# A zero fill in pieces, late expert rows copied by ScalarE, and slots moved by one

## The reference

```
# layer 0: every token against every text token, through a tanh of 256 features
h   = tanh(text @ Ws + ln(x) @ W + b)          # [b, 1024, 77, 256]
rho = h . w ; att = softmax(rho + mask)
x   = x + tanh(g) * (tanh(att.text . Wcw) * ln(x) + tanh(att.text . Wcb))
x   = x + tanh(g) * (ln(x) @ (W + low rank).T + b)
# layer 1: attention of 16 heads over the text, then a mixture of experts
x   = x + tanh(g) * (softmax(q k / 4) v @ Wo)  # q from ln(x), k and v from text
r   = top 4 of 16 experts by sigmoid(ln(x) @ router), in the 2 best of 4 groups
x   = x + tanh(g) * (sum over r of tw * (silu(x Wg) * (x Wu)) Wd  + shared expert)
```

## Time and profile before

| | us |
|---|---|
| median of 3 runs | 1641.26 (1637.31 to 1642.3) |
| profiled execution | 1636.88 |
| its span | 1635.1 |
| TensorE busy | 1297.0 (79%) |
| ScalarE busy | 1061.4 (65%) |
| VectorE busy | 979.4 (60%) |
| GpSimd busy | 593.8 (36%) |
| the chain that ended last: TensorE, VectorE, ScalarE, issue, GpSimd, DMA | 36%, 24%, 16%, 8%, 7%, 6% |

### The profile page before, as it was taken

One profiled execution on the slowest core, in us unless ns is written; L12 is line 12 of the kernel. 1 busy time (PEld: TensorE's weight loads), 2 busy tenths in 40 slices (PEclk: granted clock), 3 DMA queues, 4 the chain that ended last, 5 costly groups with the idle time before them and its releaser, 6 DMA issues.

```text
span 1635.1 us, 34527 instructions
## 1 busy us (share of the span) xinstructions
PE 1297.0 (79%) x11876; PEld 763.6 (47%) x11876; DVE 979.4 (60%) x2357; ACT 1061.4 (65%) x1739; POOL 593.8 (36%) x557
## 2 busy tenths in 40 slices
PE   4776377787579989997899889968998787688860
PEld 2211033133134745564556455646476576467750
DVE  7896137644864476458744785598438858223433
ACT  3999376997569979887699788966984241122110
POOL 2100021022273221233732435328335562735536
PEclk9877688899689999999999999999999999899995
DMA  6757700000123353244443544534437655559974
GB/s 180 226 193 183 171 1 26 14 13 27 33 91 78 104 131 98 71 117 123 149 92 107 141 148 127 135 104 141 110 92 184 170 123 137 167 138 229 253 207 119
DMA packets 227796, 202.55 MB, mean 124 GB/s; under 512 B 116747, under 2 KB 185523, under 8 KB 227635
## 3 DMA queue, kind: packets, MB, share of 16 engines
q1 hardware_dynamic: 215347, 166.78, 38.6%
q0 software_dynamic: 12288, 33.57, 6.7%
HBM read 107.49 MB, written 67.63 MB: 107 GB/s over the span
## 4 chain that ended last, share of the span: by engine, by line
PE 36%; DVE 24%; ACT 16%; issue 8%; POOL 7%; DMA 6%; SPq 3%; POOLq 0%; ACTq 0%; DVEq 0%
ACT tanh_tiles L1135 12%; PE psF L907 7%; PE psE L758 3%; PE psE L760 3%; PE psE L759 3%; DMA w_scan<-w_split 2%; DVE xc L1466 2%; POOL xs_rows L717 2%; PE psF L764 2%; PE psY L758 2%; DVE xn L1323 2%; PE psF L758 2%; DVE stats L1297 2%; PE psY L760 2%; PE psY L759 2%
## 5 line engine op out<-in xcount | busy, mean ns | idle before, releaser
L1135 ACT ACTIVATE tanh_tiles<-feat,text_bias 128x512 f32<-128x512 f32 x1232 | 771.4, 713 | 95.0 <-PE psF L907 51.6
L907 PE MATMUL psF<-tanh_tiles,wslide 128*32 128x512 f32 x2464 | 376.5, 670 | 59.9 <-ACT tanh_tiles L1135 59.3
L696 POOL TENSOR_TENSOR hid<-tile,hid 128x512 f16<-128x512 f32 x128 | 149.3, 1166 | 446.3 <-ACT hid L1154 445.9
L1514 DVE TENSOR_TENSOR tile<-tile,psE 128x512 f32<-128x512 f32 x128 | 87.4, 683 | 222.4 <-ACT tile L1162 184.8
L744 POOL TENSOR_TENSOR work<-work 128x512 f16<-128x512 f32 (+1 forms) x80 | 94.9, 1191 | 226.9 <-DVE work L1648 226.9
L758 PE MATMUL psY<-down,hid 128*128 128x256 f16 x512 | 141.9, 277 | 32.2 <-POOL hid L696 21.5
L1154 ACT CAST hid<-tile 128x512 f16<-128x512 f32 x128 | 78.4, 613 | 132.1 <-DVE tile L1514 69.6
L717 POOL DMA_INDIRECT xs_rows<-xs,slot_i x128 | 127.4, 995 | 83.8 <-issue 75.5
L758 PE MATMUL psE<-xg,gate_hi 128*128 128x128 f16 x768 | 143.7, 222 | 13.9 <-DVE tile L1514 7.7
L758 PE MATMUL psE<-xg,up_hi 128*128 128x128 f16 x768 | 149.4, 223 | 2.6 <-ACT tile L1162 2.4
L759 PE MATMUL psE<-xg,up_hi 128*128 128x128 f16 x768 | 149.1, 223 | 0.0
(11 more groups left out here) (300 smaller groups left out, 2871.2 us busy)
## 6 DMA issues: line engine op xcount, KB each, us to landing
down<-down_split SPq DMA_DIRECT2D x208, 256.0 KB, 2.7
y_rows<-hid SPq DMA_DIRECT2D x96, 256.0 KB, 3.4
xs_rows<-peakT SPq DMA_DIRECT2D x2, 6144.0 KB, 47.6
down_split<-hid SPq DMA_DIRECT2D x18, 256.0 KB, 3.1
xscan<-in_x SPq DMA_DIRECT2D x8, 512.0 KB, 4.9
x<-in_x SPq DMA_DIRECT2D x8, 512.0 KB, 4.7
w_lin<-w_split SPq DMA_DIRECT2D x15, 256.0 KB, 3.7
w_scan<-w_split SPq DMA_DIRECT2D x14, 256.0 KB
```

The source lines that it names most:

```text
L696: pool.tensor_tensor(hid_lo[:, n], tile[:, v.n % 2], hid_hi[:, n], ALU.subtract).then_inc(glo_done, 1)
L907: last = pe.matmul(psF[32 * j:32 * j + 32, RHO, :], wslide[:, c, 31 - g:63 - g], tanh_tiles[:, st.at(SETS, 2 * g + c) % HRING, j], start=g ...
L1135: act.activation(tanh_tiles[:, n % HRING, j], feat[:, c], ACT.Tanh, bias=text_bias[:, c, col:col + 1]).then_inc(h_ready, 1)
L1514: dve.tensor_tensor(tile[:, n], tile[:, n], psE[:, (2 * v.n + 1) % 3], ALU.mult).then_inc(g_done, 1)
```

## The change

- **Zero fill.** The two DMAs ahead of the slots are gone. In step 1 (first tensor) and step 2 (second) SyncE issues a twelfth every fourth slot. The first scatter of a group waits for its tensor alone.
- **Late units.** Routed units that begin in step 8 or later are copied out of PSUM by ScalarE, into a ring of four buffers made of the third tanh buffer. HIGH no longer waits for their stores. A semaphore of its own (`y_kept`) counts them; `FREED` tells TensorE which semaphore frees a PSUM bank. The ring of gathered rows shrinks from eight to six buffers.
- **Three buffers** instead of two for `slot_i` and `wk`; `place` waits for the adds of one group less.
- **Slots.** The lists of slots and lags below. The tanh of the four gains moves from before the first tanh set to before the seventh.

```diff
 SOFT, FILM, KV, KVN, X1, LN2, LN2T, LIN, LN3, LN3T, QPROJ, PEAK, PEAKT, SCORES, PV, OT, WO, LN4, LN4T, ROUTE = (
-    1, 4, 6, 5, 8, 9, 12, 14, 15, 18, 20, 22, 30, (31, 36), (35, 41), 42, 44, 45, 48, 50)
+    1, 5, 7, 5, 6, 7, 12, 13, 14, 18, 20, 22, 30, (31, 36), (35, 40), 42, 43, 45, 48, 50)
-CHOOSE = 3
+CHOOSE = 4
-PRELUDE = [48, 49, 51, 53, 53]
+PRELUDE = [48, 49, 51, 52, 53]
-BUSY = (LN2T, LN3T, QPROJ, SCORES[0], SCORES[0] + 1, SCORES[0] + 2, SCORES[1], SCORES[1] + 1, OT, LN4T, PRELUDE[2])
-BUSY1 = (2, 5, LN2T, PEAK, PEAK + 2, PEAK + 4, PEAK + 6, SCORES[0], SCORES[0] + 1, SCORES[0] + 2, SCORES[1] + 1)
+BUSY = (10, 12, 18, 20, 31, 32, 33, 36, 37, 42, 48)
+BUSY1 = (2, 12, 22, 24, 26, 28, 29, 31, 32, 33, 37)
-SCATTER = 5
+SCATTER = 6
-SILU, PROD, HIGH, LOW, DOWN, ADD, KEEP, STORE = 1, 2, 4, 5, 8, 9, 11, 12
+SILU, PROD, HIGH, LOW, DOWN, ADD, KEEP, STORE = 1, 2, 3, 5, 8, 9, 10, 11
+A_LN2T, A_LN3T, A_OT, A_LN4T, A_Q, A_PEAKT, A_SC = 0, 0, 0, 0, 1, 0, 0
+D_LN2T, D_LIN, D_LN3T, D_Q, D_QLO, D_PEAK, D_SC, D_PV, D_OT, D_WO, D_LN4T = 0, 1, 0, 1, 1, 0, 0, 0, 1, 1, 0
+P_SC = 1
-ROWS_RING = 8
+ROWS_RING = 6
+PIECES = 12
...
+        v.late = v.routed and v.at >= LATE
+LATE = STEPS * SLOTS
...
-            zeros = peakT[2 * 32:P, :].unsqueeze(1)
-            for rows in xs_dram:
-                sp.dma_start(rows.rearrange("(n p) c -> p n c", p=P // 2),
-                             zeros.to_broadcast([P // 2, ROWS_G // (P // 2), 2 * D])).then_inc(zero_filled, 16)
+            def zero_piece(n, m):
+                zeros = peakT[2 * 32:P, :].unsqueeze(1)
+                rows = ROWS_G // PIECES
+                sp.dma_start(xs_dram[n][m * rows:(m + 1) * rows].rearrange("(n p) c -> p n c", p=P // 2),
+                             zeros.to_broadcast([P // 2, rows // (P // 2), 2 * D])).then_inc(zero_filled, 16)
...
+                if s in (1, 2) and i % 4 == 0 and i // 4 < PIECES:
+                    zero_piece(s - 1, i // 4)
...
-                            pool.wait_ge(zero_filled, 32)
+                            pool.wait_ge(zero_filled, 16 * PIECES * (g + 1))
...
-                        if old.routed:
+                        if old.routed and not old.late:
                             act.wait_ge(y_stored[n], old.stored)
...
+                v = began(T, KEEP)
+                if v and v.late:
+                    if v.kept == 1:
+                        act.wait_ge(rho_part, STEPS * SETS)
+                    before = [w for w in UNITS if w.late and w.n < v.n and w.n % 4 == v.n % 4]
+                    if before:
+                        act.wait_ge(y_stored[v.n % 4], before[-1].stored)
+                    act.wait_ge(y_ps, v.y_ps[1])
+                    act.copy(y_rows(v), psY[:, v.bank % 2]).then_inc(y_kept, 1)
...
-                    dve.wait_ge(added, CHUNKS * (g - 1))
+                if g >= 3:
+                    dve.wait_ge(added, CHUNKS * (g - 2))
...
-                if v and v.routed:
+                if v and v.routed and not v.late:
                     keep_rows(v)
```

More of the change, by code:

```diff
@@ L114 @@
     stored: int = 0
+    late: bool = False
+    kept: int = 0
 def plan():
@@ L152, in plan @@
             y_ps += 2
-        if v.routed:
+        if v.late:
+            y_kept += 1
+            v.kept = y_kept
+            freed.append((True, y_kept))
+        elif v.routed:
             y_used += 1
             v.y_used = (y_used,)
-            stored[n % 4] += 16
-            v.stored = stored[n % 4]
+            freed.append((False, y_used))
         elif v.f:
@@ L160, in plan @@
             y_used += 2
+            freed += [(False, y_used - 1), (False, y_used)]
+        if v.routed:
+            stored[n % 4] += 16
+            v.stored = stored[n % 4]
     assert nxt == [NPAIR] * GROUPS
-    return units
-UNITS = plan()
+    return units, freed
+LATE = STEPS * SLOTS
+UNITS, FREED = plan()
 START = {v.at: v for v in UNITS}
@@ L350, in build, with y_rows @@
         owner = work[0:1, p0 + 608:p0 + 608 + BLOCKS]
-        rows_ring = [tanh_tiles[:, n // 2, 2 * (n % 2):2 * (n % 2) + 2].rearrange("p a (k d) -> p (a k) d", k=2) for n in range(6)]
+        rows_ring = [tanh_tiles[:, n // 2, 2 * (n % 2):2 * (n % 2) + 2].rearrange("p a (k d) -> p (a k) d", k=2) for n in range(2 * (HRING - 1))]
         rows_ring += [xscan[:, :, :], feat[:, :, :].rearrange("p c (k d) -> p (c k) d", k=2)]
+        y_late = [tanh_tiles[:, HRING - 1, n] for n in range(4)]
+        def y_rows(v):
+            return y_late[v.n % 4] if v.late else y_out[v.n % 4]
         stage = [tile[:, n, :] for n in range(2)]
@@ L458, in chunk_due, with buffer, add_lag @@
         def chunk_due(i, s, lag):
-            g, c = (s - 6) // 2, (i - lag) // COMB
-            due = s % 2 == 0 and 0 <= g < GROUPS - 1 and i >= lag and (i - lag) % COMB == 0 and c < CHUNKS
-            return (g, c, g * CHUNKS + c) if due else None
-        def gathers_before(n):
-            return TOPK * (n // ROWS_RING - 1)
-        def add_lag(s):
-            return COMB - 2 if s == 6 else ADD_LAG
+            for g, (start, every) in enumerate(COMB_AT):
+                late = s * SLOTS + i - start - lag(g)
+                if late >= 0 and late % every == 0 and late // every < CHUNKS:
+                    return g, late // every, g * CHUNKS + late // every
+            return None
+        def gathers_before(n):
+            return TOPK * ((n - CHUNKS) // ROWS_RING)
+        def buffer(n):
+            return (n - CHUNKS) % ROWS_RING
+        def add_lag(g):
+            return COMB - 2 if g == 0 else ADD_LAG
         def kv_stage(i, sc, st):
@@ L601, in slot @@
                 if v and v.routed:
-                    sp.wait_ge(y_used, v.y_used[0])
+                    if v.late:
+                        sp.wait_ge(y_kept, v.kept)
+                    else:
+                        sp.wait_ge(y_used, v.y_used[0])
                     rows = y_dram[v.g][v.pair * 2 * P:(v.pair + 1) * 2 * P, :].rearrange("(b p) d -> p b d", p=P)
-                    sp.dma_start(rows, y_out[v.n % 4].rearrange("p (b d) -> p b d", b=2)).then_inc(y_stored[v.n % 4], 16)
+                    sp.dma_start(rows, y_rows(v).rearrange("p (b d) -> p b d", b=2)).then_inc(y_stored[v.n % 4], 16)
+                if s in (1, 2) and i % 4 == 0 and i // 4 < PIECES:
+                    zero_piece(s - 1, i // 4)
                 if sc and 1 <= sc.t < STEPS - 1 and i == (44 if sc.t == STEPS - 2 else 3):
@@ L867, in down_part @@
                 if bank >= 2 and (b == 0 or not v.routed):
-                    pe.wait_ge(y_used, bank - 1)
+                    late, count = FREED[bank - 2]
+                    if late:
+                        pe.wait_ge(y_kept, count)
+                    else:
+                        pe.wait_ge(y_used, count)
                 n = v.entries[b if v.routed else 0]
@@ L1465, in add_rows @@
                 for k in range(TOPK):
-                    last = dve.scalar_tensor_tensor(out=dst, in0=rows[:, k], scalar=wk[:, g % 2, c, k:k + 1], in1=dst,
+                    last = dve.scalar_tensor_tensor(out=dst, in0=rows[:, k], scalar=wk[:, g % 3, c, k:k + 1], in1=dst,
                                                     op0=ALU.mult, op1=ALU.add)
```

101 lines of the change are left out of this document (53 added, 48 removed).

## The result

The kernel before took 1639.28 us (median of 4 runs, 1636.66 to 1642.3), the changed kernel 1578.44 us (median of 4, 1577.42 to 1583.24). The ratio is 0.9634, interval 0.9606 to 0.9662: 3.7% faster, 60.8 us. The prediction was 1587 us with a range of 1560 to 1613. The profiled execution took 1577.42 us, with a span of 1575.7, against 1636.88 and 1635.1.

A forecast was written before the change was run, and what follows sets the result against it. Step 1 stalls on query weights behind the zero fill; tanh steps nearly fill TensorE and ScalarE, then routed experts set the pace. Terms -25.7 - 14 - 6 - 7 = -52.7 from 1636.88 give 1584.2, plus 3: 1587 us, range 1560 to 1613.

The forecast's parts named there:

- Zero fill, -25.7 us: Step 1: fill in pieces ends TensorE's wait for w_scan before the query projection; -25.7 us, bounds -27 and -10.
- Slots, -14 us: Tanh steps 2 to 7: moved tanh set 7.5 us plus fewer transpose waits 6 us; bounds -35 and +15.
- The 7.5 us for the tanh set moved out of slot 10: Steps 2, 4 and 6: tanh activations moved into ScalarE's boundary hole save about 2.5 us each.
- The 6 us for X1 and LN2 ahead of other work of VectorE: Steps 2 to 7: earlier X1 and LN2 save a tenth of ScalarE's 57.5 us of transpose waits.
- HIGH, 0: Routed units: ScalarE's cast one slot earlier costs nothing, since 3.5 us of slack covers the 2.56 us taken.
- Rival (c): Steps 3 to 7: earlier HIGH makes ScalarE wait 0.7 us per unit, 52 us back, 1654 us; chance 0.05.
- Late copies, -6 and -7 us: Copies moved to ScalarE save 6 us in step 8; ended y_rows waits save 7 us in steps 9 and 10.
- End, 0: Final gathers and adds: six buffers instead of eight cost nothing, as the first adds come well before the last gathers.
- Rival (a): Only the zero fill pays, steps worth 0 and the late part 3 us; 1611 us, chance 0.26.
- (d): Step 1: SyncE's bursts of pieces before loads leave only 10 us won, 3 us elsewhere; 1627 us, chance 0.06.
- (b): The steps pay in full, -27 - 25 - 12 - 12 = -76 us, giving 1564 us; chance 0.15.
- signs of being wrong: A new wait over 0.5 us per unit before the hid cast, or steps moving over 6 us each either way.

The follow-up runs named there:

- two other kernels with the same instructions in step 1: Changed kernel with VectorE copying all routed results, ratio 0.9706; changed kernel with five low halves on VectorE and a later scatter wait, 0.9592.
- the first and the third series: Timing sessions of four experiments each, with ratios to the kernel before on the same chip, which took 1670 us in the first and 1641 us in the third.

## Why the prediction was right, and where it was not

**Zero fill, -25.7 us.** Right in mechanism and place. The wait of 25.72 us is gone; the pieces alone gave 29 us, and putting the fill back into the changed kernel cost 20 to 26. The piece of the sum that was missing is TensorE's busy time: I held the rest of step 1 fixed at its length and named "about 129 us"; it took 124.5, because TensorE was also busy 5.9 us less. The stall explains some 2.8 us of that, the work done at the lower level right behind it. The rest can't be put down to the fill: two other kernels with the same instructions in step 1, and no stall, were busy for 95.1 us there, 0.9 less than before, and took 129.4 and 129.0 us, just what I had named. The 24 x 1.04 = 25 us that I gave as the upper end for issues was too low (the 24 issues took 31.4 us of SyncE), and nothing hung on it. Going against the Trainium skill's advice to batch 1 MiB and more per DMA ("DMA: Bandwidth & Descriptors", "Bandwidth") cost nothing here: a piece landed in 6.5 us, and at whatever rate it moved, no load on the path waited for it.

**Slots, -14 us.** Steps 2 to 7 gave -24.8 us, inside the bounds of -35 and +15, and the reasons were partly wrong. The 7.5 us for the tanh set moved out of slot 10 can't be found in the total (0.9666 against 0.9674). The boundary hole did shrink by 2.2 us, about the 2.5 that I forecast, and the kernel was not shorter for it. ScalarE's idle time at the boundary was not what the step waited for. So the parity failed too: steps 2, 4 and 6 were to be shorter by 3 to 4, steps 3, 5 and 7 by 1 to 2; they gave 3.1, 1.0, 6.2 and 4.0, 4.6, 5.9. The 6 us for X1 and LN2 ahead of other work of VectorE were the right mechanism, cut down to a tenth of ScalarE's waits for transposes with no better reason than TensorE's idle time; put back alone they cost 20 to 22 us. I also said that in steps 3, 5 and 7 the same work only stands in another order: the order was worth 10.9 us there. What I left out is that a matmul that waits for xn holds TensorE's whole queue, and that the clock can fall in such a wait: 5.3 + 2.2 us in step 6. The moves in the second half of the step, which I put at 0, go with 9 to 12 us, in step 5 nearly all of it clock. CHOOSE, SCATTER, FILM and K/V were never put back alone.

**HIGH, 0.** Right: 0.9685 against 0.9674. The slack I named was not there everywhere: the cast waits 19.5 us for VectorE in steps 3 to 7 in place of 4.5, in waits of up to 7.2 us. They cost nothing, as the pair of kernels with 18.6 and 0.7 us of them shows. Rival (c) had its wait and not its price.

**Late copies, -6 and -7 us.** Too much. To the last scatter the gain is 192.7 - 188.9 = 3.8 us, of which the late copies have 2.4 by the pair that differs in them; after it the gain is 0. I had read the 62.6 us of waits as mostly hidden, and still took 7.4 us of them, from units at 5.61 us where others took 5.04. But TensorE was busy for 129.4 of 148 us there, so that most of the 5.2 us a unit is its work, and part of its idle time lies in holes like the one of the loads behind SyncE's wait for the scatters. The wait of ScalarE changed its name, from y_rows to psE, and the time stayed. Even that change of name is not the late copies' alone: with the new slots and without them only 4.4 us of it are left.

**End, 0.** Right: 57.2 and 57.0 us, though six buffers hold the gathers in place of eight.

**The sum.** Predicted -25.7 - 14 - 6 - 7 = -52.7. Measured by the profiles -30.2 - 24.8 - 3.8 + 0.1, with -0.8 elsewhere, -59.5. Two terms were too small by 4.5 and 10.8 us, two too large by 2.2 and 7.1. The time came out 9 us from the forecast because these errors cancel in part, and that is luck. Rival (a), only the fill, fell with the 14 to 20 us of the slots; (d) with the wait of 0.42 us; (b) had the slots right at 25 us and the late part wrong. Of the signs of being wrong that I wrote down, one was just met: step 6 moved by 6.2 us, where the limit was 6.

## What to carry to other kernels

A move of one slot is worth what it changes in the waits of the engine that is nearest to full. In this kernel: look for the instruction of TensorE whose input comes late, and bring the producer forward on its engine, past work that nobody waits for yet or into its waits. Idle time of ScalarE beside it (3.4 us at each boundary, 18 us before the hid cast, 60 us for stores) paid nothing that the totals show when it went. Where a stall of TensorE goes, compare its busy time before and after for the same matmuls: part of the gain, or of an unexplained loss, can be clock, and that part differs by some us between kernels with the same code.

## What the runs showed of the hardware

Step 1 with the same instructions took 124.5 and 129.4 us, TensorE busy 90.2 and 95.1 us, at granted clocks of 0.88 and 0.84. The second value came up in two kernels (129.4 and 129.0 us), the first in three profiles: the changed kernel in two series (124.5 and 124.6) and the one with the unit's old slots (124.6). What decides it is open. An effect under 5 us in this kernel can't be read from one profile's total; the steps have to be read one by one.

The same two kernels took 1639 and 1578 us in one series and 1677 and 1624 us in another. It is not the chip alone: the first and the third series ran on the same one, and the kernel before took 1670 and 1641 us there. The longer traces hold 21 to 28 waits with the releaser remote, of up to 21 us, and more with issue; the shorter ones have none with remote. Their cause is open.

Where TensorE stood still, the lower level followed: from 171.7 us in a wait that began at 167.62, and from 919.2 us in one that began at 915.14. The eight transposes behind the second took 1.94 us in place of 1.06. The same low half of a unit (128x512) took 1.16 us on GpSimd and 0.69 on VectorE.
